# Routing of a mixture of experts moved ahead of its shared layers, with its scatters taken choice by choice

## The reference

```python
def ffn(x):                                # x: 1024 x 256, normed
    shared = silu_and_mul(x @ Wgu.T) @ Wd.T          # hidden 704
    shared = shared * sigmoid(x @ sgate.T)
    p = softmax(x @ gate_w.T)                        # 16 experts
    w, ids = top_k(p, 4)
    for e in range(16):
        coef = sum(where(ids == e, w, 0))
        acc += (silu_and_mul(x @ w13[e].T) @ w2[e].T) * coef   # hidden 176
    return shared + acc
x = x + A(norm(x)); x = x + ffn(norm(x)); x = x + B(norm(x)); x = x + ffn(norm(x))
```

## Time and profile before

| | us |
|---|---|
| three runs | 1356.03, 1356.97, 1358.3 (median 1356.97) |
| the profiled execution, its own time | 1354.85 |
| its span | 1352.6 (2.25 lie outside) |
| PE busy / DVE / ACT / POOL | 1218.9 / 829.8 / 817.8 / 786.4 |
| mean granted TensorE clock | 0.947 |

### The profile page before, as it was taken

The page is one execution under the profiler, slowest core; times in us unless marked ns, Lnnn a source line. Parts: engine busy times, 40 slices in busy tenths (PEclk is TensorE's granted clock), DMA queues, the critical chain, the costliest instruction groups (busy, mean ns, idle before and its releaser), DMA issues. The chain is left out here.

```text
span 1352.6 us, 23382 instructions
## 1 busy us (share of the span) xinstructions
PE 1218.9 (90%) x7476; PEld 1062.6 (79%) x7476; DVE 829.8 (61%) x2025; ACT 817.8 (60%) x1782; POOL 786.4 (58%) x657
## 2 busy tenths in 40 slices
PE   5899999999978598994999999999999986869993
PEld 4688888888856476772899999999999975657772
DVE  4767777777777142335677777777776766523332
ACT  4777877778744133332778788888878854213331
POOL 4156766667523625563667777777777741625663
PEclk8999999999979799996999999999999988969997
DMA  3155666654319537663322232212232015725665
GB/s 101 55 156 143 163 125 177 152 144 106 68 39 274 180 62 146 103 96 85 90 56 61 60 82 59 65 54 62 69 70 70 16 44 171 254 79 87 113 109 134
DMA packets 95814, 141.42 MB, mean 105 GB/s; under 512 B 8504, under 2 KB 79160, under 8 KB 93880
## 3 DMA queue, kind: packets, MB, share of 16 engines
q1 hardware_dynamic: 76896, 99.49, 28.1%
q0 software_dynamic: 16608, 21.37, 9.8%
q10 hardware_dynamic: 2232, 19.56, 4.8%
HBM read 99.72 MB, written 40.68 MB: 104 GB/s over the span
## 5 line engine op out<-in xcount | busy, mean ns | idle before, releaser
L1208 POOL DMA_INDIRECT sums_d<-e_y,xg x94 | 146.1, 1554 | 138.6 <-ACT e_y L1146 124.6
L406 POOL TENSOR_TENSOR ms_a<-m_a,ms_a 128x384 fp32r<-128x384 f32 x128 | 130.1, 1017 | 99.2 <-ACT ms_a L402 99.0
L1299 DVE COPY e_hT<-ps 88x256 f32<-88x256 f32 x94 | 39.5, 421 | 151.7 <-PE ps L1077 131.2
L1064 PE MATMUL ps<-w,e_xT 128*128 (+1 forms) x376 | 127.5, 461 | 1.0 <-ACT e_xT L1132 1.0
L833 DVE TENSOR_TENSOR m_a<-ps,e_a 128x384 f32<-128x384 f32 x128 | 71.1, 556 | 70.6 <-PE ps L272 68.1
L270 PE MATMUL ps<-xn_hi,aw_hi 128*128 128x512 f32 x256 | 107.5, 420 | 0.8 <-DVE bmat_lo L765 0.8
L272 PE MATMUL ps<-xn_hi,aw_lo 128*128 128x512 f32 x256 | 101.5, 396 | 0.0
L271 PE MATMUL ps<-xn_lo,aw_hi 128*128 128x512 f32 x256 | 101.3, 396 | 0.0
L406 POOL TENSOR_TENSOR qk_lo<-qf,qk_hi 128x512 fp32r<-128x512 f32 x64 | 84.2, 1338 | 26.6 <-ACT qk_hi L402 25.7
L1087 PE MATMUL ps<-w,e_hT 88*128 (+1 forms) x376 | 97.3, 382 | 0.0
L406 POOL TENSOR_TENSOR ms_b_lo<-m_b,ms_b_hi 128x384 fp32r<-128x384 f32 x64 | 65.3, 1020 | 52.7 <-ACT ms_b_hi L402 52.7
(11 more groups left out here) (311 smaller groups left out, 4506.6 us busy)
## 6 DMA issues: line engine op xcount, KB each, us to landing
rows_a<-a_rows_d SPq DMA_DIRECT2D x64, 256.0 KB, 5.0
xg<-slots_d SPq DMA_DIRECT2D x94, 138.0 KB
w<-moe_up ACTq DMA_DIRECT2D x8, 1408.0 KB
slots_d<-slot_init SPq DMA_DIRECT2D x10, 1104.0 KB, 7.7
wconv_raw<-b_conv SPq DMA_DIRECT2D x16, 513.0 KB, 3.6
aw_raw<-a_heads SPq DMA_DIRECT2D x32, 256.0 KB, 2.9
wvo_raw<-b_vo SPq DMA_DIRECT2D x16, 512.0 KB, 3.5
rows_b<-b_rows_d SPq DMA_DIRECT2D x32, 256.0 KB, 4.7
```

The source lines that it names most:

```text
L406: return nc.gpsimd.tensor_tensor(dst[1], src, f32(dst[0]), ALU.subtract).then_inc(sem(done_sem), 1)
L1064: ins = nc.tensor.matmul(ps[:, 2 + t % 2, 0:2 * E_HIDDEN], e_xT[:, t % 2, k], weights_of(w13, t, at_w, k * 2 * E_HIDDEN, 2 * E_HIDDEN), st ...
L1208: nc.gpsimd.indirect_dma_start(sums_d[f][t % CHAINS], bass.IndirectOffsetOnAxis(ap=xg[:, t % XG, ROW_ID:ROW_ID + 1].bitcast(U32), axis=0), ...
L1299: nc.vector.tensor_copy(e_hT[0:HALF_E, t % 2], ps[0:HALF_E, 4 + t % 2, 0:2 * P].rearrange("p (j m) -> p j m", j=2)).then_inc(sem("e_hT"), 1)
```

## The change

Routing is brought forward and its parts are reordered:
- **PE**: chunk 1 does only the gate half of up(0) before the logit transposes; the rest of up(0), then chunk 0 of up(1), then three rank matmuls (which now give ranks with the offsets of earlier blocks), down(0) chunk 0, up(1) chunk 1, the wait `ranks_read`, down(0) chunk 1.
- **ACT**: the logits of chunk 0 are copied before the norm of chunk 1 is finished. The eight weight transfers leave the head of `f_act`: four are issued after the logits of chunk 1, four behind the splits for tiles 2 and 1. The sigmoid becomes an exp on ACT and an add and a reciprocal on DVE; two small activations are added.
- **DVE**: the choice is made on the logits in PSUM; the copy `lg`, the row-max reduction and the memsets go (their constants come in `rc`, now 608 columns, 311 KB, issued by SP behind the norm). Slots are found by MAX8 over slot times mask in two halves, in place of the two 512-column operations. The choice and the slots go ahead of the other work of tiles 0 and 1. Weights are stored unnormalised with 1/sum in one more column; each expert tile multiplies by it, one more 128x1 operation for tiles 0 to 15, none for the others.
- **POOL**: token ids and a memset move to POOL. The 32 scatters go choice by choice, lowest slots first, with a semaphore for each choice.
- **SP**: tile t below 4 waits only for the first t + 1 choices. After the last tile the sums of each chain are loaded as soon as that chain has ended, and `f_last_dve` adds them one chain at a time.

```diff
--- before.py
+++ after.py
...
+        ROUTE_BANK, RANKS, COUNTS = 7, slice(2 * P, 3 * P), slice(3 * P, 3 * P + EXPERTS)
...
-            f_up_pe(pe, f, 0, [c])
+            if c == 0:
+                f_up_pe(pe, f, 0, [c])
+            else:
+                f_up_part_pe(pe, 0, c, 0)
...
+            f_up_part_pe(pe, 0, 1, 1).then_inc(sem("f_up_done"), 1)
+            f_up_pe(pe, f, 1, [0])
+
+            routed(pe, "dve", f, "sofar")
+            nc.tensor.matmul(ps[:, ROUTE_BANK, RANKS], after, mask, start=True, stop=False, skip_group_check=True)
+            nc.tensor.matmul(ps[:, ROUTE_BANK, RANKS], ones, sofar[:].rearrange("p e b -> p b e"), start=False, stop=False,
+                             skip_group_check=True)
+            nc.tensor.matmul(ps[:, ROUTE_BANK, COUNTS], ones, sofar[:, :, BLOCKS - 1], start=False, stop=True,
+                             skip_group_check=True).then_inc(sem("f_route_pe"), 1)
             f_down_pe(pe, f, 0, [0])
-
-            routed(pe, "dve", f, "mask")
-            chosen = r_gt[:].rearrange("p i e -> p (i e)")
-            nc.tensor.matmul(ps[:, 7, 0:P], tri[:], chosen, start=True, stop=True, skip_group_check=True)
-            nc.tensor.matmul(ps[:, 7, P:2 * P], ones[:], chosen, start=True, stop=True, skip_group_check=True
-                             ).then_inc(sem("f_route_pe"), 1)
-            routed(pe, "dve", f, "lg")
+            f_up_pe(pe, f, 1, [1])
             routed(pe, "dve", f, "ranks_read")
             f_down_pe(pe, f, 0, [1])
...
+        def f_up_part_pe(pe, i, c, s):
+
+            for k in range(KT):
+                ins = mm3(ps[:, 2 * s + c, :], at(fgu, slice(None), i % 2, k, s), at(xn, slice(None), k, cols(c)), k == 0, k == KT - 1)
+            return ins
+
         def f_up_pe(pe, f, i, chunks=range(CHUNKS)):
             gu_split(pe, f, i)
...
-        def f_act(act, n, f):
-            act.dma_start(rc[:], route_c).then_inc(sem("rc_loaded"), 16)
-            for g in range(W_GROUPS):
+        def f_first_act(act, f):
+
+            f_lgT_act(act, f, 0)
+            warm_act(act, ACT.Silu, 2)
+
+        def f_w_act(act, groups):
+
+            for g in groups:
                 span = slice(g * GROUP_E * E_STRIDE, (g + 1) * GROUP_E * E_STRIDE)
                 act.dma_start(w13[:, span], moe_up[:, span]).then_inc(sem(f"w_loaded{g}"), 16)
                 act.dma_start(w2[0:HALF_E, span], moe_down[:, span]).then_inc(sem(f"w_loaded{g}"), 16)
+
+        def f_act(act, n, f):
             f_silu_act(act, f, 0, 0)
-            f_lgT_act(act, f, 0)
+            warm_act(act, ACT.Exp, 3)
             f_hi_act(act, f, 0, 0)
             f_lgT_act(act, f, 1)
-            f_silu_act(act, f, 0, 1)
-            f_up_weights_act(act, f, 2)
+            f_w_act(act, range(2))
             routed(act, "dve", f, "shift")
             nc.scalar.activation(pr[:], pr[:], ACT.Exp).then_inc(sem("f_route_act"), 1)
-            nc.scalar.activation(sg[:], lg[:, :, GATE_ROW], ACT.Sigmoid).then_inc(sem("f_route_act"), 1)
+            nc.scalar.activation(sg[:], sg[:], ACT.Exp).then_inc(sem("f_route_act"), 1)
+            f_silu_act(act, f, 0, 1)
             f_hi_act(act, f, 0, 1)
+            f_up_weights_act(act, f, 2)
             f_down_weights_act(act, f, 1)
+            f_w_act(act, range(2, W_GROUPS))
...
+            normed(pool, n)
+            nc.gpsimd.memset(rows[:, :, ROW_NORM + 1:], 0.0)
+            nc.gpsimd.tensor_copy(rows[:].bitcast(I32)[:, :, ROW_ID], tokid[:]).then_inc(sem("pool_made"), 1)
             f_split_gu_pool(pool, f, 2)
             f_split_d_pool(pool, f, 1)
+            pool.wait_ge(sem("pool_made"), POOL_MADE["ids"] + f)
             pool.wait_ge(sem("slots_ready"), 16 * len(INITS))
-            routed(pool, "dve", f, "slots")
-            for b in range(BLOCKS):
-                for k in range(TOP_K):
+            for i, k in enumerate(reversed(range(TOP_K))):
+                for b in range(BLOCKS):
+                    if i == 0 and b % CHUNK_BLOCKS == 0:
+                        routed(pool, "dve", f, f"slots{b // CHUNK_BLOCKS}")
                     nc.gpsimd.indirect_dma_start(slots_d[f], bass.IndirectOffsetOnAxis(ap=slot4_i[:, b, k:k + 1], axis=0),
-                                                 rows[:, b, :], None).then_inc(sem("slots_stored"), 16)
+                                                 rows[:, b, :], None).then_inc(sem(f"slots_stored{i}"), 16)
...
             f_lo_dve(dve, f, 0, 0)
             routed(dve, "pe", f, "lg_T")
-            nc.vector.tensor_copy(lg[:], ps[:, 6, 0:BLOCKS * LOGITS].rearrange("p (i e) -> p i e", e=LOGITS)
-                                  ).then_inc(sem("f_route_dve"), 1)
-            routed(dve, "dve", f, "lg")
-            step(nc.vector.tensor_reduce(r_mx[:], lg[:, :, 0:EXPERTS], AX_X, ALU.max))
-            nc.vector.tensor_tensor(pr[:], lg[:, :, 0:EXPERTS], r_mx[:, :, None].broadcast_to(R_WIDE),
-                                    ALU.subtract).then_inc(sem("f_route_dve"), 1)
+            lg = ps[:, ROUTE_BANK, 0:BLOCKS * LOGITS].rearrange("p (i e) -> p i e", e=LOGITS)
+            f_choose_dve(dve, f, lg, step)
             f_h_dve(dve, f, 0, 1)
-            f_choose_dve(dve, f, step)
+            f_slots_dve(dve, f, step)
             f_lo_dve(dve, f, 0, 1)
-            f_h_dve(dve, f, 1, 0)
-            f_lo_dve(dve, f, 1, 0)
-            f_slots_dve(dve, f, step)
-            f_h_dve(dve, f, 1, 1)
-            f_lo_dve(dve, f, 1, 1)
+            for c in range(CHUNKS):
+                f_h_dve(dve, f, 1, c)
+                f_lo_dve(dve, f, 1, c)
             f_split_d_dve(dve, f, 2)
             f_split_gu_dve(dve, f, 3)
             f_tiles_dve(dve, f, step)
+            routed(dve, "act", f, "sg")
+            step(nc.vector.tensor_scalar(sg[:], sg[:], 1.0, None, ALU.add))
+            step(nc.vector.reciprocal(sg[:], sg[:]))
...
-                c = xg[:, t % XG, ROW_PR + t:ROW_PR + t + 1]
+                dve_step(dve, nc.vector.tensor_tensor(c, xg[:, t % XG, ROW_PR + t:ROW_PR + t + 1], norm, ALU.mult))
             else:
-                c = coef[:, t % 2:t % 2 + 1]
                 dve_step(dve, nc.vector.tensor_tensor_reduce(coef_x[:, t % 2], xg[:, t % XG, ROW_PR:ROW_PR + EXPERTS],
-                                                             one_hot[:, t - EXPERTS], 1.0, 0.0, ALU.mult, ALU.add, c))
+                                                             one_hot[:, t - EXPERTS], norm, 0.0, ALU.mult, ALU.add, c))
...
-        def f_last_dve(dve, n, f, c):
-            dve.wait_ge(sem(f"sums_loaded{c}"), 16 * CHAINS * (f + 1))
-            for q in range(CHAINS):
-                for b in range(2 * c, 2 * c + 2):
-                    ins = nc.vector.tensor_tensor(of_batch_x(b), of_batch_x(b), sums[:, q, HALF * b:HALF * (b + 1)], ALU.add)
-                    if q == CHAINS - 1:
-                        ins.then_inc(sem(f"x_updated{n + 1}"), 1)
-                if q < CHAINS - 1:
-                    dve_step(dve, ins)
+        def f_last_dve(dve, n, f, i, c):
+
+            dve.wait_ge(sem(f"sum{i}_loaded{c}"), 16 * (f + 1))
+            for b in range(2 * c, 2 * c + 2):
+                ins = nc.vector.tensor_tensor(of_batch_x(b), of_batch_x(b), sums[:, ENDED[i], HALF * b:HALF * (b + 1)], ALU.add)
+                if i == CHAINS - 1:
+                    ins.then_inc(sem(f"x_updated{n + 1}"), 1)
+            if i < CHAINS - 1:
+                dve_step(dve, ins)
...
-        def f_choose_dve(dve, f, step):
-
-            routed(dve, "act", f, "exp")
+        def f_choose_dve(dve, f, lg, step):
+
+            logits = lg[:, :, 0:EXPERTS]
             for b in range(BLOCKS):
-                ins = nc.vector.max(out=r_top[:, b], in_=pr[:, b])
+                ins = nc.vector.max(out=r_top[:, b], in_=lg[:, b, 0:EXPERTS])
             step(ins)
-            least = r_top[:, :, TOP_K - 1:TOP_K].broadcast_to(R_WIDE)
-            nc.vector.tensor_tensor(r_gt[:], pr[:], least, ALU.is_gt)
-            step(nc.vector.tensor_tensor(r_eq[:], pr[:], least, ALU.is_equal))
-
+            most, least = (r_top[:, :, k:k + 1].broadcast_to(R_WIDE) for k in (0, TOP_K - 1))
+            nc.vector.tensor_tensor(r_gt[:], logits, least, ALU.is_gt)
+            nc.vector.tensor_tensor(r_eq[:], logits, least, ALU.is_equal)
+            nc.vector.tensor_scalar(sg[:], lg[:, :, GATE_ROW], -1.0, SIGMOID_BOUND, ALU.mult, ALU.min)
+            nc.vector.tensor_tensor(pr[:], logits, most, ALU.subtract).then_inc(sem("f_route_dve"), 1)
+            routed(dve, "dve", f, "shift")
...
+            step(nc.vector.tensor_tensor(mask, r_gt[:], r_eq[:], ALU.add))
+            nc.vector.tensor_tensor_scan(flat(sofar), keep_eb, flat(mask_eb), 0.0, ALU.mult, ALU.add).then_inc(sem("f_route_dve"), 1)
+
+            routed(dve, "act", f, "exp")
+            step(nc.vector.tensor_reduce(r_sum[:], pr[:], AX_X, ALU.add))
+            nc.vector.reciprocal(rows[:, :, ROW_NORM], r_sum[:])
```

(87 more changed lines are left out.)

117 lines of the change are left out of this document (34 added, 83 removed).

## The result

The changed kernel takes 1347.26 us (median of 8) against 1357.63 for the kernel before: ratio 0.9922, interval 0.9906 to 0.9938. The forecast was 1325; the direction is right, the size is a third of the 32 us foreseen. The profiled execution has a span of 1342.5.

A forecast was written before the change was run, and what follows sets the result against it. PE bounds the kernel, the 32 scatters' end its slow stretch. 2 x 13 (crawl) + 4 + 2 (sums) = 32; 1354.85 - 32 + 2.1 = 1325 us; own range 1315 to 1337, 8 in 10 1304 to 1353.

The forecast's parts named there:

- Crawl after: Before the experts: if it needs the weights' ring dry, 8 us from about 1182 to 1190; 13 us gained per call.
- The crawl: PE's matmuls of down(3) come one at a time, released by "issue", 1178.0 to 1200.4; 20.1 us lost.
- two things that coincide at the crawl's start: At the start of PE's slow stretch: 18 scatters issued, and the expert weights' ring q10 run dry.
- Rival B: The crawl follows the scatters, only moving to 1168 to 1190; gain 6 from the sums, 1351; chance 0.24.
- Routing sooner: Second call's routing: logits 3.3 us sooner, first scatter at 1144.5, 10.5 us earlier.
- up(3): Shared stage: starts at 1162.4 again, held by tile 3's weight load; gain taken as 0, bounds 3.6 gained to 1 lost.
- Weights: Expert weights start later and end at 1183 to 1190; experts need them from about 1200: hidden.
- Rival D: Scatters stretch tile 3's load to 19.1 us, up(3) 6.4 us later in both calls; 1364; chance 0.10.
- Rival C: No crawl, the weights' ring never being dry before the scatters land; gain 50 us, 1307; chance 0.15.
- Sums: After the last scatter-add: loads and adds shorter by 4 us in the second call, 2 in the first.
- Expert stage: One added 128x1 DVE operation for 16 tiles costs nothing; bounds 0 to 2.6 us per call, taken as 0.

The follow-up runs named there:

- set 4: Runs on one chip where nothing crawls: the kernel before took 1333.37 us, the changed kernel 1308.61, ratio 0.9821.
- b1: The kernel before with only the last edit (each chain's sums loaded and added as soon as that chain has ended): ratio 0.9959.
- e2: The changed kernel with POOL pausing between the 16th and 17th scatter until PE has done down(2): 1327.87 us, ratio 0.9807.
- c3: The kernel before with POOL pausing after its 16th scatter until PE has done down(3), on a chip with the crawl: ratio 0.9912.
- e3: The changed kernel with one matmul instead of three in each product of shared tiles 2 to 5, at lower precision: 1319.06 us, one run.

## Why the prediction was wrong

**The step that failed** is "Crawl after. If it needs the weights' ring dry, it runs from about 1182 or not at all": 8 us long, 8.9 lost, 13 gained per call. The crawl doesn't need the ring dry. It began with q10 at work, 26 to 29 us after the first scatter in both calls, at 1166.2 + 6.5 = 1172.7 in the second, and ended 4 us after the last scatter was issued. Measured there are 19.0 us for 14 matmuls worth 1.9 (12 at 0.12, 2 at 0.23), so 17.1 lost in it, and 1.7 at the low clock behind it: 18.8 in place of the 8.9 forecast, where the kernel before lost 22.2. Of the 3.4 us so gained the low clock in up(3) took 2.3 back. Experts were reached 485.95 - 483.22 = 2.7 us sooner in the first call and 7.8 - 6.5 = 1.3 in the second (1206.3 for 1214.1), not 13. I had named two things that coincide at the crawl's start and chosen one with no more evidence than for the other. Rival B (it follows the scatters, 1351) was the right one, its figure 4 us off; the measured time lies in the range of 1304 to 1353 only because that took rival B in.

**Routing sooner: right.** DVE had the logits at 1135.3 in the clock of before, and the first scatter came 8.6 sooner for 10.5; the two collisions with POOL took 1.4 of the rest. But what that is worth depends on what it uncovers: without a crawl it takes away PE's waits of 9.09 and 8.26 us (with the 5.5 of the sums 22.9 of the 24.8 us of set 4), with one it moves the crawl from down(3) to down(2).

**up(3): right on its start, not on its price.** It did not move, as forecast: PE's 3.56 us wait went, and PE idled 6.34 us before up(3) instead. I took 0 for this; the low clock that followed the idle time cost the 2.3 us named above.

**Weights: right that they are hidden.** The ring was done by about 1176 (1182.5 in the clock of before, for 1183 to 1190), and the expert stage has PE full (115.83 of 116.70 us).

**Rival D:** there was no sign of it; up(3) was 0.7 late, not 6.4. **Rival C's** 1307 is what the changed kernel takes where nothing crawls (1308.6), but that is luck: the kernel before has no crawl there either.

**Sums: size nearly right.** Loads and adds after the last scatter-add are 4.0 shorter in the second call, as forecast, but that scatter-add lands 9.95 us after PE's last expert group instead of 8.83, so 2.9 stay. In the first call it is 1.6 for 2 (PE's wait for the norm is 15.05 instead of 16.64). b1 alone gave 5.5.

**Expert stage: right within 0.6 in the second call,** 116.4 us for 115.8. In the first it is 1.5 shorter, which no run explains.

Total by the traces: 2.7 + 1.3 from the shared stages, 1.6 + 2.9 from the sums, about 1.6 from the rest, 10.1 in the spans.

**Open:** what fills or is held up. Shown is that, on three chips of five, a long stream of scatters brings it; that a pause in the stream mostly takes it away; that the number of rows doesn't matter; that a dry weights' ring is neither needed (the changed kernel) nor enough (e2); and that it is over 3 to 6 us after the last scatter is issued. Not shown is a count at which it sets in: with the stream unbroken it began 22 to 30 us after the first scatter, with 17 to 23 issued, in c3 after 15 us with 12. The late signals, which come first and are there in e3 without a crawl, suggest that PE's signals are held up and PE itself only when enough of them stand in line; no experiment tested this. Chip and moment are not parted, as no chip was measured twice. All runs here are traced, so whether the crawl exists without the profiler is open too.

## What to carry to other kernels

When two things coincide at the start of a stall, price the change by both and let the worse one into the forecast, however neat the other is. Where an engine crawls with "issue" as its releaser, look also at the engines that wait for it: a late "remote" release there shows the same state, even in a run whose own pace looks healthy (e3). Then try to break up the stream beside it: one wait in POOL's stream of 32 scatters gave 15 to 19 us on top of the change, where the crawl exists. Such a fix is not free elsewhere (two pauses cost 5 us without the crawl, and one in the old kernel 7), so measure on more than one chip.
